# Windowed attention scores as 64x64 tiles of TensorE, with plain 128x512 copies of the transposed queries

## What is computed

```python
# DEPTH = 6, HEADS = 16, DIM_HEAD = 64, WINDOW = 32
def attn_layer(x, Wqkv, qs, ksc, Wo):
    q, k, v = split(x @ Wqkv)                    # 16 heads of 64
    q, k = l2norm(q) * qs, l2norm(k) * ksc       # then rotary, with decay
    sim = einsum('bhwie,bhwje->bhwij', bq, bk2) * 8.0   # 32 queries against own and previous window
    sim = where(mask, -max, sim)
    out = einsum('bhwij,bhwje->bhwie', softmax(sim), bv2)
    return out @ Wo
for i in range(6):
    x = attn_layer(shift_tokens(x), ...) + x
    x = ffn_layer(shift_tokens(x), ...) + x
```

## Time and profile before

| | us |
|---|---|
| median of 3 runs | 6488.89 |
| lowest and highest | 6476.83, 6489.27 |
| the profiled execution | 6469.97 |
| its span, first to last instruction | 6468.2 |
| mean granted TensorE clock | 0.908 |

### The profile page before, as it was taken

One profiled execution on the slowest core, in us unless ns is written; L12 is line 12 of the kernel. 1 busy time (PEld: TensorE's weight loads), 2 busy tenths in 40 slices (PEclk: granted clock), 3 DMA queues, 4 the chain that ended last, 5 costly groups with the idle time before them and its releaser, 6 DMA issues. The chain is left out here.

```text
span 6468.2 us, 131403 instructions
## 1 busy us (share of the span) xinstructions
PE 5368.8 (83%) x35512; PEld 4551.3 (70%) x35512; DVE 4714.4 (73%) x12576; ACT 3761.0 (58%) x12063; POOL 2034.1 (31%) x1699
## 2 busy tenths in 40 slices
PE   5986959971899978999689996999969999699994
PEld 4665948971777757777577775777757777577773
DVE  4553757775777777777777777877778777778777
ACT  1112424330777747777477773777737777377772
POOL 0000000001444424444244442444424444244441
PEclk7886969995999989999899998999979999799997
DMA  0001200001000011000100001000010000100001
GB/s 18 0 0 27 51 1 0 0 0 36 23 21 21 22 39 25 22 19 21 43 22 22 22 22 42 22 21 20 22 42 22 22 22 19 42 22 21 22 22 47
DMA packets 103763, 146.40 MB, mean 23 GB/s; under 512 B 65414, under 2 KB 72859, under 8 KB 103131
## 3 DMA queue, kind: packets, MB, share of 16 engines
q1 hardware_dynamic: 94155, 109.63, 7.5%
q0 software_dynamic: 9232, 33.12, 1.6%
HBM read 49.13 MB, written 2.10 MB: 8 GB/s over the span
## 5 line engine op out<-in xcount | busy, mean ns | idle before, releaser
L1463 POOL TENSOR_TENSOR d_qk<-d_qk,d_sin_terms 128x512 f32<-128x512 f32 x792 | 994.5, 1278 | 1626.0 <-DVE d_sin_terms L1898 1626.0
L1781 ACT ACTIVATE d_probs<-d_S_ps,d_neg_max 128x96 f32<-128x96 f32 x3096 | 1010.8, 342 | 235.0 <-DVE d_neg_max L1927 233.1
L1469 POOL TENSOR_TENSOR d_qk<-d_qk,d_inv_norm 128x1024 f32<-128x1024 f32 x396 | 745.2, 1903 | 606.8 <-DVE d_inv_norm L1921 606.8
L1576 PEld LDWEIGHTS d_S_ps<-d_kT,d_q_blocks 128*128 128x128 f32 x6240 | 836.2, 199 | 5.5
L1898 DVE TENSOR_TENSOR d_qk<-d_A_ps,d_tables 128x512 f32<-128x512 f32 x816 | 564.4, 692 | 377.5 <-ACT d_squares L1744 371.5
L1576 PE MATMUL d_S_ps<-d_kT,d_q_blocks 128*128 128x96 f32 x6240 | 833.9, 278 | 0.0
L1781 ACT ACTIVATION_READ_ACCUMULATOR d_probs<-d_S_ps,d_neg_max 128x1 f32 x3096 | 643.3, 208 | 0.0
L1533 PE MATMUL d_A_ps<-d_wqkv_hi,d_xT_hi 128*128 128x512 f32 x1212 | 591.5, 488 | 14.6 <-DVE d_sin_terms L1898 9.9
L1890 DVE TENSOR_REDUCE d_sum_squares<-d_squares 128x16 f32<-128x1024 f32 x402 | 488.6, 1215 | 127.3 <-issue 121.2
L1540 PE MATMUL d_T_ps<-d_ident,d_qk 128*128 128x128 f32 x3168 | 495.9, 280 | 94.4 <-POOL d_qk L1469 90.1
L1898 DVE TENSOR_TENSOR d_sin_terms<-d_A_ps,d_tables 128x512 f32<-128x512 f32 x816 | 555.5, 681 | 0.0
(11 more groups left out here) (392 smaller groups left out, 11394.0 us busy)
## 6 DMA issues: line engine op xcount, KB each, us to landing
d_v_early<-d_v SPq DMA_DIRECT2D x198, 256.0 KB, 3.0
d_v_early<-d_v SPq DMA_DIRECT2D x198, 128.0 KB, 2.3
d_tables<-L_ffn_rotary POOLq DMA_DIRECT2D x7, 2048.0 KB, 9.7
d_qk<-L_ffn_Wqkv POOLq DMA_DIRECT2D x21, 512.0 KB, 4.1
d_xs<-d_xb SPq DMA_DIRECT2D x96, 63.5 KB
d_xs<-d_xb SPq DMA_DIRECT2D x48, 127.0 KB
ax_fp_blocks<-L_ffn_blocks_gu SPq DMA_DIRECT2D x16, 256.0 KB, 3.9
ax_fp_scales<-L_ffn_scales_gu SPq DMA_DIRECT2D x64, 64.0 KB, 3.4
```

Of the source, the lines that this page charges most:

```text
L1463: nc.gpsimd.tensor_tensor(c4[:, :, s, :], c4[:, :, s, :], s4[:, :, 1 - s, :], ALU.add).then_inc(rotated, 1)
L1469: nc.gpsimd.tensor_tensor(r3, r3, rn[:, b, k, :].unsqueeze(2).broadcast_to([P, HEADS, HD]), ALU.mult).then_inc(scaled, 1)
L1576: last = nc.tensor.matmul(S[g % 2][:, n * SEEN:(n + 1) * SEEN], qx[:, p, half, :], kT[b][jj][:, p, HALF * half:HALF * half + SEEN], start= ...
L1781: nc.scalar.activation(pr[:, g, n, seen_columns(g)], S[g % 2][:, n * SEEN:(n + 1) * SEEN], ACT.Exp, bias=nmax[:, g, n:n + 1], accum_out=de ...
```

## The change

For each head apart, the scores are now computed with weights of 64x64 (the 64 queries of that head) and moving data of 64x96. Head one uses partitions 0 to 63 of the operands and writes partitions 0 to 63 of the bank; head two uses and writes 64 to 127. In the built program these matmuls have a tile size of 64x64, at tile positions (0, 0) and (64, 64). There are eight in a call where there were four. The queries need no block diagonal any more: `qT` holds the transposed queries as they come (128 x 8 x 128), one copy of 128x512 per half writes it, and one semaphore, `q_T_ready`, stands in the place of `q_T_low` and `q_T_high`. The memset of `q_blocks` goes. The mask matmul ahead of the heads stays as it is, and so does all else.

```diff
-        qx = m.sb("q_blocks", [P, PAIRS, 2, P])
+        qT = m.sb("qT", [P, PAIRS, P])
...
-                nc.gpsimd.memset(qx[:].rearrange("p c s t -> p (c s t)"), 0.0).then_inc(init, 1)
...
                     if g % 2 == 0:
-                        pe.wait_ge(q_T_low, f * 2 + (2 + g // 2))
-                        pe.wait_ge(q_T_high, f * 2 + (2 + g // 2))
+                        pe.wait_ge(q_T_ready, f * 2 + (2 + g // 2))
                         pe.wait_ge(k_T_ready, f * 2 + (1 + g // 2))
...
                     for n in range(UNITS):
                         p, half = unit(g, n)
-                        last = nc.tensor.matmul(S[g % 2][:, n * SEEN:(n + 1) * SEEN], qx[:, p, half, :],
-                                                kT[b][jj][:, p, HALF * half:HALF * half + SEEN], start=False,
-                                                stop=True, skip_group_check=True)
+                        for head in range(2):
+                            rows = slice(HD * head, HD * head + HD)
+                            last = nc.tensor.matmul(S[g % 2][rows, n * SEEN:(n + 1) * SEEN], qT[rows, p, HALF * half:HALF * half + HALF],
+                                                    kT[b][jj][rows, p, HALF * half:HALF * half + SEEN], start=False,
+                                                    stop=True, skip_group_check=True)
                     last.then_inc(scores_ps, 1)
...
                 def drain_q_T(f, half):
                     act.wait_ge(qk_T_ps, f * 4 + (half + 3))
-                    nc.scalar.activation(qx[0:HALF, 4 * half:4 * half + 4, :, 0:HALF],
-                                         T0[0:HALF, :].rearrange("p (c s t) -> p c s t", c=4, s=2), ACT.Copy
-                                         ).then_inc(q_T_low, 1)
-                    nc.scalar.activation(qx[HALF:P, 4 * half:4 * half + 4, :, HALF:P],
-                                         T0[HALF:P, :].rearrange("p (c s t) -> p c s t", c=4, s=2), ACT.Copy
-                                         ).then_inc(q_T_high, 1)
+                    nc.scalar.activation(qT[:, 4 * half:4 * half + 4, :], T0[:].rearrange("p (c t) -> p c t", c=4), ACT.Copy
+                                         ).then_inc(q_T_ready, 1)
```

More of the change, by code:

```diff
@@ L1271, in windowed_transformer @@
         k_T_ready, k_T_before = m.sem("k_T_ready"), m.sem("k_T_before")
-        q_T_low, q_T_high = m.sem("q_T_low"), m.sem("q_T_high")
+        q_T_ready = m.sem("q_T_ready")
         early_dma = [m.sem(f"early_dma{b}") for b in range(B)]
@@ L1545, in transpose_k @@
                         pe.wait_ge(k_scaled, f + 1)
-                        pe.wait_ge(q_T_low, f * 2 + 1)
-                        pe.wait_ge(q_T_high, f * 2 + 1)
+                        pe.wait_ge(q_T_ready, f * 2 + 1)
                     else:
@@ L1558, in transpose_q @@
                     else:
-                        pe.wait_ge(q_T_low, f * 2 + 2)
-                        pe.wait_ge(q_T_high, f * 2 + 2)
+                        pe.wait_ge(q_T_ready, f * 2 + 2)
                     transpose_four(0, half)
@@ L1677, in _ @@
                     pe.wait_ge(resid_a, (l + 1) * (U * 2) + 2)
-                    pe.wait_ge(q_T_low, (l + 1) * (FRONTS * 2) + 1)
-                    pe.wait_ge(q_T_high, (l + 1) * (FRONTS * 2) + 1)
+                    pe.wait_ge(q_T_ready, (l + 1) * (FRONTS * 2) + 1)
                     pe.wait_ge(max_done, (l + 1) * SCORES_IN_LAYER)
@@ L1800, in _ @@
                 nc.scalar.nop().then_inc(o_low, 1)
-                nc.scalar.nop().then_inc(q_T_low, 1)
-                nc.scalar.nop().then_inc(q_T_high, 1)
+                nc.scalar.nop().then_inc(q_T_ready, 1)
                 with act.Fori(0, DEPTH) as l:
```

## The result

The changed kernel takes **6517.48 us** (median of 6 runs, 6508.4 to 6526.8) against 6488.86 us for the kernel before (6 runs, 6475.7 to 6490.04): ratio 1.005, 95% interval 1.0035 to 1.0064. It is slower, by 29 us and not by 104. The profiled execution took 6517.1 us, with a span of 6515.2.

A forecast was written before the change was run, and what follows sets the result against it. TensorE bounds half two of each unit, VectorE's chain half one: two calls at +0.385 us (+0.77) less 0.23 from the copies, +0.54 us times 192 units = +104 us, giving 6593 us; range 6470 to 6800.

The forecast's parts named there:

- the loads overlap as well: Rival for the scores calls: both tiles' loads and matmuls overlap, a call +0.175 us, +23 us in all, 6512; chance 0.17.
- the copies: ScalarE's query copies, one per half for two: the residual add begins earlier, 0.23 us per unit gained, 44 us.
- Loads set the pace and the two tiles' matmuls overlap: First of three values for a scores call's body: 15 loads at 0.057 us, +0.07 us; the one taken.
- the third value: Scores call's body: matmuls and loads of the two tiles both overlap, 0.63 us, so -0.14.
- In and out: TensorE drains switching between full-size and 64x64 matmuls: +0.145 us into a call, +0.17 out.
- Which half pays: Of a unit's four scores calls, two are hidden in half one's stalls; two in half two cost +0.77 us.
- half two: Unit's stretch from the first transpose of k to the next output projection's end; TensorE sets its pace; calls g=0, g=1.
- half one: Unit's stretch from output projection's end to first transpose of k, paced by VectorE's chain; calls g=2, g=3; loses 0.23 us.
- The rival that ScalarE was the bound: Rival: ScalarE bounds the kernel, so its saved 1.20 us per unit came back; no chance given.
- taking turns: Rival in the scores calls: the tiles don't overlap, a call +0.765 us, +271 us in all, 6760; chance 0.22.
- no drain: Rival: no drain between full-size and tiled matmuls; -17 us (6472), or -98 us (6391) with overlapping loads; chance 0.12.
- a drain at each head: Rival: seven more drains of about 0.2 us in each call, over 700 us slower; given little chance.

The follow-up runs named there:

- E3: Changed kernel with each call's matmuls grouped, all of head one, then all of head two, tiles not alternating: 6747.01 us, 1.0407 of the kernel before.
- E5: Changed kernel with 64x64 tiles only in the calls g=0 and g=1, full weights in the others (scores mixed there): 6515.4 us, 1.0057 of the kernel before.
- E6: Changed kernel with 64x64 tiles only in the calls g=2 and g=3, full weights in the others (scores mixed there): 6462.87 us, 0.9977 of the kernel before.
- E1: Changed kernel with 128x128 weights again, the single 128x512 copy per half kept (scores mix two heads): 6457.93 us, 0.9974 of the kernel before.
- E2: Changed kernel with 64x64 tiles kept, but queries copied in two 64x512 instructions per half: 6519.07 us, 1.0066 of the kernel before.
- E10: Kernel before (two copies, full weights), with g=0 and g=1 scores merged into one call after attend 3 and g=3's projection: 6543.06 us, 1.0101 of before.
- E4: Changed kernel with head two's score matmuls left out, so half of the scores are missing: 6573.56 us, 1.0152 of the kernel before.

## Why the prediction was wrong

The direction was right, the size was not: +104 us were forecast and +29 came, near where the rival "the loads overlap as well" had put it (+23, 6512). That rival had the mechanism of the tiles right, but it is luck that its time came so close: it had a call at 0.175 us where 0.11 was measured, and the copies at 0.23 us a unit where 0.07 was. Two terms of the forecast's sum were mis-sized, in opposite directions.

**The body of a call: the failed step.** "Loads set the pace and the two tiles' matmuls overlap" put the body, from a call's first matmul to its last, at +0.07 us. In fact the loads of two tiles overlap like the matmuls: in the trace two loads start 7 ns apart, and then two matmuls 7 ns apart. By the medians of the 192 calls of g=1 the body went from 0.753 us (forecast 0.77) to 0.635: **-0.12**, where the third value, "the tiles overlap and their loads do too", had put -0.14. The second pair follows the first after 0.13 us, as long as its load takes; from there on a pair, one matmul of each head, comes every 0.083 us, against 0.112 for the full-size matmul. The pace is that of a matmul alone; the load of 64 columns hides behind it, as the load of 128 did not. The reason given for the first value, that "loads follow one another in every row of this trace", spoke of loads into one and the same tile. E3 shows the condition: it is the order of the program in which the tiles must alternate. The Trainium skill's rule in TensorE: Matmul & The Clock Gate, Part 3 (matmuls of different row groups about 4 ns apart) held here, with 7 ns. The Trainium skill's TensorEngine Tiling, Gotcha 1 (row tiles can't access one PSUM bank together) did not show in these two tiles, which write different quadrants of one bank. What the prediction took from the Trainium skill's PSUM — Partial Sum Buffer (PSUM bank collisions) on different quadrants is stated there for accesses of two different engines; that two tiles of TensorE may do it too is what these runs show.

**In and out: right in kind, each somewhat too dear.** The first load starts 0.26 us after the start of the mask matmul (2523.80 to 2524.06), as forecast; its matmul starts with it and not 0.05 later, so the way in is +0.09 (0.173 to 0.267 us from mask to heads) instead of +0.145. Out, before and then after:

```profile
2527.05 0.28 PE L1576 MATMUL d_S_ps<-d_kT,d_q_blocks 128*128 128x96 f32 x1
2527.16 0.41 PE L1608 MATMUL d_PT_ps<-d_wo,d_attnT 128*128 128x128 f32 x2
```
```profile
2524.69 0.25 PE L1574 MATMUL d_S_ps<-d_kT,d_qT 64*64 64x96 f32 x2
2524.87 0.38 PE L1606 MATMUL d_PT_ps<-d_wo,d_attnT 128*128 128x128 f32 x1
```

From the last matmul of the heads to the first of the output projection it is 0.11 us before and 0.17 after (medians 0.112 and 0.173): +0.06, not +0.17, because here too the first matmul starts with its load and not 0.107 behind it. The second matmul pays instead, with its load no longer ahead: 0.213 us behind the first where it was 0.138, so the output projection takes 1.81 us instead of 1.74, another +0.07. Sum: 0.09 - 0.12 + 0.06 + 0.07 = **0.11** by the unrounded medians, where 0.385 stood. (The forecast's body, 0.855 less 0.77, is 0.085 and not 0.07; the slip is worth some 5 us of the total.)

**Which half pays: right.** E5 and E6 show it without rest: 2 x 0.11 = 0.22 us per unit, all of it from half two.

**The copies: the mechanism was right, its size was not.** With d = 0.11, under the break-even of 0.115 that the prediction named, its own sum would give no change. It is slower because the copies give 0.07 us and not 0.23. The add does start as soon as the output projection is done,

```profile
2507.08 0.23 DVE L1941 TENSOR_TENSOR d_xs<-d_PT_ps,d_xs 128x64 f32 x1 [0.65 <-PE d_PT_ps L1606]
2507.22 0.22 DVE L1942 TENSOR_TENSOR d_xb<-d_PT_ps,d_xb 128x64 f32 x1
2507.45 1.22 DVE L1882 TENSOR_REDUCE d_sum_squares<-d_squares 128x16 f32<-128x1024 f32 x1
```

and VectorE waits for TensorE now, where it came late by itself at 2509.80. But the signal takes 0.16 us (L1606 ends at 2526.92 in the next unit, the add starts at 2527.08), not the 0.05 allowed; so 0.12 of 0.28 is gained. Then, at the end of one of the two units at the upper level (the third of the four), the sum of squares follows the second add after 0.23 us (above) instead of 0.13 as at the end of the fourth and before, which takes 0.10 back; why, the trace does not say, and it was not tried. That agrees with E1, where the third unit gains 0.01 us and the fourth 0.13. Half one is another 0.11 shorter up to the transposes of k (L1517 to L1539 3.90 us at the median of the third units, before 4.01), in E1 and E2 too, and this is lost right behind them: `attend` 1 now waits for ScalarE's copy of the probabilities,

```profile
2533.73 0.60 ACT L1782 ACTIVATE d_probsT<-d_PT_ps 128x512 f32<-128x512 f32 x1
2533.75 0.65 PE L1539 MATMUL d_T_ps<-d_ident,d_qk 128*128 128x128 f32 x4 [0.29 <-POOL d_qk L1468]
2534.38 0.49 PE L1597 MATMUL d_O_ps<-d_probsT,d_v 128*128 128x128 f32 x2
```

which started 0.12 before these transposes in the kernel before and starts with them now: `attend` 1 follows them after 0.63 us, where it was 0.52. The prediction stopped its half one at the transposes of k and did not ask what is late next.

Together +0.22 - 0.07 = +0.15 us, times 192 = 29 us. The two parts are not quite independent: in E2, with two copies, the add starts 0.16 us behind the output projection as well, because the output projection itself ends later there. Beside the tiles the single copy is worth only 0.04 us a unit (19.87 / 19.88 in E2 against 19.79 / 19.88), and the tiles alone cost 0.19 of their 0.22. The rival that ScalarE was the bound fell (E1: 230 us of ScalarE's work less, 19 us gained), and so did taking turns, no drain and a drain at each head.

## What to carry to other kernels

Two small tiles on the diagonal of the array cost as much as one, if they alternate in the program; what costs is each change between tile sizes, here 0.25 us with its way back. So gather the small matmuls before making them small: merging two calls turned +0.5% into -0.4% (of which E1 puts 0.26 down to the plain copies, which the tiles make possible). And cost a merged or moved block by what it lets come earlier, too: the queue that now arrives last (in E10, by its waits, ScalarE's) decides whether the order pays.

## What the hardware showed that was not expected

- Leaving out half of a TensorE phase made the kernel slower. The work's length did not change (0.80 us a call), while the stretches at the 1.2 GHz level after the loop's turn grew from mostly 3.4 or 6.8 to 10.2 us (E4), and so did they in E3, whose work was all there but took longer. What makes them grow stays open.
- Loads into different tiles overlap as matmuls do: 16 loads of 64 columns take 0.69 us, and two start 7 ns apart.
- A full-size fp32 matmul of 96 columns is paced by its load (0.1125 us), so the same work in two tiles, a pair every 0.084 us, runs a quarter faster once inside.
